# A fused recurrent, feed-forward and attention block on one core: a negative mean for GpSimd, five small loads on another queue, the weight preparation on VectorE, and a new plan

## The chip, the core and the metric

The kernel runs on one core of a Trainium2 chip. The core has five engines that work side by side: TensorE (PE, matrix products; its weight loads are shown as PEld), VectorE (DVE), ScalarE (ACT), GpSimd (POOL) and SyncE (SP), which here only issues transfers. The metric is the device time of one execution in microseconds (us): 1856.88 us is the median of three executions before the change (1855.34 to 1861.38).

## The reference

x has 4096 tokens of 256 channels in float32. Four residual layers follow one another, each on a layer-normalized x:

```
x = x + A(ln(x)); x = x + F(ln(x)); x = x + B(ln(x)); x = x + F(ln(x))

A(x): i, f, o = sigmoid(x Wi + bi), sigmoid(x Wf + bf), sigmoid(x Wo + bo);  s = tanh(x Ws + bs)
      h_t = f_t * h_(t-1) + i_t * s_t           (a scan over all 4096 tokens, per channel)
      z = x + o * h;  A = (z - mean z) / sqrt(var z + eps) * gamma + beta
F(x): p = x of the token before (0 for the first)
      r = sigmoid((mu_r x + (1 - mu_r) p) W_r);  k = (mu_k x + (1 - mu_k) p) W_k
      F = r * (relu(k)^2 W_v)
B(x): q, k, v = x Wq' + bq, x Wk' + bk, x Wv' + bv;  16 heads of 16 channels
      causal softmax(q k' / 4) v per head, over all earlier tokens;  B = that Wo' + bo
```

## The kernel before

The first three layers' token-wise part and the attention run interleaved. A **unit** is 256 tokens (16 of them, `UNIT`), a **chunk** 512 tokens (8). Each unit goes through normalization LN_X, the gates f, i, s, o, the scan, the normalization LN_Z, the first feed-forward (LN_F1) and the projections to q, k and v (LN_A); this is called the front here. Attention goes over 32 **steps**, four groups of four heads for each chunk. A step has two passes over its keys. In the first one (`max`), TensorE makes the scores of 128 queries against up to 512 keys and VectorE reduces each to its maximum (L1284). In the second one (`scores`, L1510), the scores come again with the maximum subtracted by two additional rows of the product (`shift`, `place`), ScalarE takes the exponential (`exp`, L1069) and TensorE adds up the values (`pv`, L1531). A step's scores can't begin before all its maxima are known. After a chunk's four steps its two units get the output projection and the second feed-forward (LN_F2).

**The order of the work** on each engine is written out when the program is built. `schedule()` plays the whole kernel through with a table of costs (`COST`), of landings (`LANDS`, `LOADED`) and with weights (`WORTH`) by which TensorE chooses between a maximum, a score, a `pv` and a product of a unit (`job`). An engine then executes its instructions in that fixed order and waits on semaphores for what they need. `MAX_AHEAD` and `AHEAD` say how far the maxima may run ahead of the scores (in steps, and in key columns; all maxima together have 540,672 columns). `LEAD` says how far the load of a unit may run ahead of the attention: `may_begin` lets the load of unit u start when the position in chunks plus LEAD plus 1 has reached u/2. `MOST` says how many of the seven PSUM banks each kind may hold.

**A normalization** (`normalize`, L843 to L848) has VectorE make mean and variance (L1143, L1158); GpSimd then makes rstd = (var + eps)^-0.5 in two small instructions (L840, L841, each waited for) and applies `(x - mean) * rstd` in two instructions of 128x256 (L846). For the first `EARLY` = 2 units of the front, and the last `LATE` = 2 of the second feed-forward, GpSimd makes only rstd and VectorE applies it (`apply` L1178, `z.apply` L1188 and L1194); for their feed-forward VectorE also subtracts (L1206) and accumulates (L1211), and ScalarE squares (L1023), where GpSimd does these three for the other units (L927, L937, L932).

**The preparation** is done once. GpSimd waits until all 15 transfers of `rest_loaded` have landed (the weights v, q, k, r, k of the feed-forward, v and o of the attention, five vectors of 256, and three broadcast rows), halves the weight w_v (L858), makes 1 - mu_r and 1 - mu_k (L860), bv as columns (L863) and the squares of the q and k weights (L866). TensorE sums the squares (L1452, `bound`) and makes the product of bv with w_ao (L1459, `bo`), VectorE adds that to bo (L1122, `bo.add`) and makes from the sums a scale for q and k (`scale.bound`, `scale.apply`). At the start SyncE's queue issues x of unit 0, the gate weights, two further units of x, then the other weights and rows. ScalarE's queue issues four gate biases, gamma and beta, and then the five vectors bq, bk, mu_r, mu_k and bv (L959) before ScalarE's first instruction.

Of the kernel before, what the change touches and what calls it, by code (L numbers as in the profile page):

```python
# [59 lines left out]
MOST = {"max": 4, "scores": 5, "job": 4}  # L60
# [9 lines left out]
EARLY = 2  # L70
# [3 lines left out]
def at_ends(u, ln):  # L74
    return u >= UNITS - LATE if ln == LAST else u < EARLY

# [6 lines left out]
          for a in range(0, (c * TT + qt + 1) * P, SPAN)]  # L83
# [3 lines left out]
AHEAD = 2212205  # L87
LEAD = 1.5
SOON, TWO = 0, -1300
REDUCE, EXP = 600, 480  # L90
WORTH = {"max": 2400, "dve": 1.0, "scores": 2650, "act": 1.562, "half": 450, "pv": 750, "stay": -4750, "two":
         -650, "ring": 900, "last": -2850, "job": 900, "age": 0.021, "same": 750, "after": -900, "rest": 450}
# [11 lines left out]
    "DVE": {"ln.stats": 660, "ln.mean": 140, "is": 620, "scan": 1320, "y": 700, "z": 620, "mixk": 750, "mixr": 750,  # L104
            "r*kv": 620, "q.part1": 800, "kk.part1": 800, "x3": 620, "neg": 230, "part0": 180, "part1": 180,
            "recip": 190, "norm": 350, "halve": 300, "scale.bound": 2300, "scale.apply": 3500,
            "bo.add": 400, "apply": 500, "z.apply": 1600, "subtract": 620, "accumulate": 620},
    "POOL": {"ln.norm": 2300, "z.norm": 4900, "rstd": 1100, "f.affine": 600, "x+beta": 1290, "diff": 1250, "k2": 1050,
             "x2": 1290, "x2+bo": 1290, "mask": 650, "scale.raise": 1100, "prev": 250, "consts": 6500, "prepare": 5000},
# [6 lines left out]
LOADED = {"halve": 9000.0, "f": 10000.0, "prepare": 20000.0}  # L116
# [6 lines left out]
def followed():  # L123
# [26 lines left out]
    op(("prepare",), ("consts",))  # L150
    op(("bound",), ("prepare",))
# [5 lines left out]
    for u in range(UNITS):  # L157
# [46 lines left out]
        for f in (FIRST, LAST):  # L204
# [18 lines left out]
            op(("kv", u, f, 0), ("square" if at_ends(u, f) else "k2", u, f), *so_on("kv", u - 1, f, 1))  # L223
# [32 lines left out]
def schedule():  # L256
# [15 lines left out]
    def offer(k):  # L272
        ready[engine[k[0]]][k] = max([seen[a] for a in after[k]] + [LOADED.get(k[0], 0.0)])

# [256 lines left out]
def build(nc, x, Wi, bi, Wf, bf, Wo_gate, bo_gate, Ws, bs, gamma, beta, WqT, bq, WkT, bk, WvT, bv, WoT, bo,  # L531
          WrT, WkfT, WvfT, mu_r, mu_k, out):
    with ExitStack() as ctx:
# [24 lines left out]
        small = sb("small", [P, 4 * 3 + 2 + 5 * UT * (6 + 2 + 2) + UT + CT * 3])  # L558
# [3 lines left out]
        var_eps, rstd = (small[:, 14 + n * UT:14 + (n + 5) * UT].rearrange("p (l t) -> p l t", l=5) for n in (40, 45))  # L562
        minus_half = small[:, 14 + 50 * UT:14 + 51 * UT]
        h_last = small[:, 14 + 51 * UT:14 + 51 * UT + CT].rearrange("p (k a) -> p k a", a=1)
# [144 lines left out]
        def _(sp):  # L709
# [8 lines left out]
            for n, w in (("v", WvfT), ("aq", WqT), ("ak", WkT), ("r", WrT), ("k", WkfT), ("av", WvT), ("ao", WoT)):  # L718
                matrix(n, w, rest_loaded)
# [851 lines left out]
```

## Time and profile before

| | |
|---|---|
| time, median of three | 1856.88 us |
| the profiled execution, its own time | 1857.59 us |
| its span, first to last instruction | 1855.9 us |
| busy, of the span | PE 1749.0 (94%), DVE 1583.7 (85%), ACT 1312.5 (71%), POOL 530.3 (29%) |
| granted TensorE clock, mean | 0.985 |

The time outside the span is 1.7 us. A row of a timeline has the start in us from the span's start, the length in us of the instructions merged in it, engine, line, operation, output and input, and in brackets the idle time of the engine just before and what ended it. An engine's name with a q (ACTq, SPq) is its queue issuing transfers. A busy PE is not a PE at its peak, since the ends of its products are modelled.

### The profile page before, as it was taken

How to read it: one execution, taken by the hardware profiler on the slowest of the kernel's cores; microseconds unless marked ns; L12 is line 12 of the kernel's file. 1: busy time of each engine (PE TensorE's matmuls, PEld its weight loads, DVE VectorE, ACT ScalarE, POOL GpSimd, SP SyncE). 2: the span in 40 equal slices, each digit the busy share in tenths (PEclk: the TensorE clock that was granted, in tenths of full speed). 3: DMA queues.
4: the chain of work that ended last, by engine and by line, in shares of the span. 5: the costliest groups of instructions: out<-in, count | busy, mean ns of one | idle time of the engine just before them, and what ended most of it. 6: DMA issues, size and time to landing. Idle time of an engine off the chain costs nothing.

```text
span 1855.9 us, 34235 instructions
## 1 busy us (share of the span) xinstructions
PE 1749.0 (94%) x12684; PEld 755.4 (41%) x12684; DVE 1583.7 (85%) x3175; ACT 1312.5 (71%) x2757; POOL 530.3 (29%) x655
## 2 busy tenths in 40 slices
PE   6689999999999999999999999999999999999997
PEld 5565546354444343353443333433432233332224
DVE  4566789897989998999999999999999999999802
ACT  2235474647676877748778878788778888888893
POOL 5556645544432232432213022131110001110001
PEclk9988999999999999999999999999999999999998
DMA  3131202121020000020002000000110000000000
GB/s 105 40 63 33 50 19 49 38 41 34 16 51 12 20 15 23 12 46 12 28 17 34 6 1 17 28 1 6 33 25 5 6 4 3 13 1 7 1 1 12
DMA packets 56954, 42.99 MB, mean 23 GB/s; under 512 B 8788, under 2 KB 56788, under 8 KB 56788
## 3 DMA queue, kind: packets, MB, share of 16 engines
q1 hardware_dynamic: 53188, 39.74, 8.8%
q10 hardware_dynamic: 3600, 1.06, 0.4%
q8 instruction: 101, 1.65, 0.4%
q14 instruction: 65, 0.53, 0.1%
HBM read 24.00 MB, written 16.25 MB: 22 GB/s over the span
## 4 chain that ended last, share of the span: by engine, by line
PE 29%; DVE 22%; ACT 6%; POOL 3%; issue 2%; DVEq 0%; POOLq 0%; ACTq 0%
DVE span_max L1284 19%; PE psum L1531 9%; PE psum L1510 6%; PE psum L1478 5%; ACT probs L1069 5%; PE psum L1347 4%; PE psum L1341 3%; POOL rows L846 1%; PE psum L1335 1%; DVE rows L1252 1%; DVE small L1143 0%; POOL small L841 0%; PE psum L1540 0%; PE psum L1485 0%; POOL probs L953 0%
## 5 line engine op out<-in xcount | busy, mean ns | idle before, releaser
L1284 DVE TENSOR_REDUCE span_max<-psum 128x1 f32<-128x512 f32 (+3 forms) x2304 | 1312.7, 635 | 73.4 <-PE psum L1478 36.4
L1069 ACT ACTIVATE probs<-psum 128x512 f32<-128x512 f32 (+3 forms) x2304 | 1115.5, 596 | 204.1 <-PE psum L1510 200.8
L1531 PE MATMUL psum<-probs,v_aug 128*17 128x512 f32 (+3 forms) x4608 | 569.2, 566 | 5.8 <-POOL probs L953 4.3
L1478 PE MATMUL psum<-k_stack,q_stack 48*128 48x512 f16 (+3 forms) x2304 | 520.0, 364 | 15.5 <-DVE span_max L1284 8.9
L1510 PE MATMUL psum<-q_stack,k_stack 50*128 50x512 f16 (+3 forms) x2304 | 515.5, 367 | 6.5 <-ACT probs L1069 1.5
L1510 PEld LDWEIGHTS psum<-q_stack,k_stack 50*128 50x128 f16 x2304 | 137.5, 93 | 510.9 <-ACT probs L1069 440.4
L953 POOL TENSOR_SCALAR_AFFINE_SELECT probs<-probs 128x512 f32<-128x512 f32 x128 | 82.0, 643 | 603.0 <-ACT probs L1069 602.9
L1478 PEld LDWEIGHTS psum<-k_stack,q_stack 48*128 48x128 f16 x2304 | 165.1, 94 | 197.4 <-DVE span_max L1284 111.3
L846 POOL TENSOR_SCALAR rows<-rows,small 128x256 f32<-128x256 f32 x140 | 174.3, 1253 | 7.4
L1531 PEld LDWEIGHTS psum<-probs,v_aug 128*17 128x17 f32 x4608 | 76.6, 95 | 137.6 <-issue 112.7
L995 ACT ACTIVATE rows<-psum,cols 128x256 f32<-128x256 f32 x128 | 53.6, 470 | 83.7 <-PE psum L1341 83.2
L937 POOL TENSOR_TENSOR rows<-rows 128x512 f32<-128x512 f32 x28 | 35.5, 1268 | 193.8 <-DVE rows L1261 193.8
L1485 PE MATMUL psum<-mask_keys,mask_rows 64*128 64x64 bf16 x1024 | 90.2, 190 | 0.0
L1143 DVE BATCH_NORM_STATS2 small<-rows 128x6 f32<-128x256 f32 x160 | 59.5, 414 | 33.9 <-POOL rows L906 23.7
L1335 PE MATMUL psum<-ident,rows 128*128 128x128 f32 x256 | 42.7, 294 | 47.1 <-POOL rows L846 23.1
L1485 PEld LDWEIGHTS psum<-mask_keys,mask_rows 64*128 64x128 bf16 x1024 | 74.7, 97 | 29.8 <-issue 0.8
L1341 PE MATMUL psum<-rows,w_k 128*128 128x256 f32 x256 | 73.0, 410 | 8.0 <-DVE rows L1252 6.6
L932 POOL TENSOR_TENSOR rows<-rows 128x512 f32<-128x512 f32 x28 | 29.6, 1058 | 170.7 <-ACT rows L1017 170.7
L1308 DVE RECIPROCAL inv_sum<-psum 128x16 f32<-128x16 f32 x32 | 8.1, 253 | 78.6 <-PE psum L1540 78.2
L1036 ACT ACTIVATE rows<-psum,cols 128x256 f16<-128x256 f32 x64 | 26.8, 471 | 64.0 <-PE psum L1341 63.8
L1347 PE MATMUL psum<-w_r,rows 128*128 128x256 f32 x256 | 70.4, 399 | 1.6 <-DVE span_max L1284 0.9
L1347 PE MATMUL psum<-w_v,rows 128*128 128x256 f32 x256 | 69.7, 396 | 2.1 <-POOL rows L932 0.7
(118 smaller groups left out, 1347.7 us busy)
## 6 DMA issues: line engine op xcount, KB each, us to landing
q_stack<-q_parts SPq DMA_DIRECT2D x192, 32.0 KB, 2.0
k_stack<-k_parts SPq DMA_DIRECT2D x42, 128.0 KB, 4.8
rows<-in_x SPq DMA_DIRECT2D x16, 256.0 KB, 3.0
q_parts<-rows SPq DMA_DIRECT2D x32, 128.0 KB, 1.9
k_parts<-rows SPq DMA_DIRECT2D x32, 128.0 KB, 2.0
out<-rows SPq DMA_DIRECT2D x16, 256.0 KB, 2.2
x_rows<-rows SPq DMA_DIRECT2D x14, 256.0 KB, 2.1
rows<-x_rows SPq DMA_DIRECT2D x14, 256.0 KB, 2.8
```

The source lines that it names most:

```text
L846: ins = nc.gpsimd.tensor_scalar(dst[:, j], src[:, j], mean_var[:, ln, j, 0:1], rstd[:, ln, j:j + 1], ALU.subtract, ALU.mult)
L953: nc.gpsimd.affine_select(out=tri, in_=tri, compare_op=ALU.is_ge, fill=0.0, base=0, pattern=[[0, HG], [1, P]], channel_multiplier=-1).then ...
L1069: act.activation(probs[:, tile % PROBS, i, q0:], bank(b)[:, q0:], ACT.Exp, scale=SCALE / QK_SCALE).then_inc(exp_done, 1)
L1143: ins = nc.vector.bn_stats(stats[:, ln, j], src[:, j])
L1284: nc.vector.tensor_reduce(span_max[:, s % SPAN_RING, row:row + 1, k0 // SPAN:k0 // SPAN + 1], bank(b)[:, 0:k1 - k0], AX.X, ALU.max).then_i ...
L1335: ins = nc.tensor.transpose(bank_chan(b)[:, k, j * P:(j + 1) * P], src[:, j, k * P:(k + 1) * P], ident[:])
L1341: ins = nc.tensor.matmul(bank_chan(b)[:, e], w[:, k, e * P:(e + 1) * P], src[:, k], start=(k == 0), stop=(k == CT - 1))
L1347: ins = nc.tensor.matmul(bank_tok(b)[:, j], src[:, k, j * P:(j + 1) * P], w[:, k], start=(k == 0), stop=(k == CT - 1))
L1478: ins = nc.tensor.matmul(bank(b)[:, 0:k1 - k0], q_stack[row:row + SCORE_ROWS, s % Q_RING, u, qt * P:(qt + 1) * P], k_stack[row:row + SCORE ...
L1485: ins = nc.tensor.matmul(bank(b)[:, k:k + HALF], mask_rows[row:row + HALF, n], mask_keys[row:row + HALF], start=False, stop=(n == 1))
L1510: nc.tensor.matmul(bank(b)[:, q0:], k_stack[row:row + STACK, g * PAIRS + u, j * P:(j + 1) * P], q_stack[row:row + STACK, s % Q_RING, u, q0 ...
L1531: ins = nc.tensor.matmul(pv_bank[32 * h:32 * h + VW, q0:], v_aug[:, j, g * HG + h, :], probs[:, tile % PROBS, h, q0:], start=(j == 0), sto ...
```

## The change

It has seven parts. (1) GpSimd's `normalize` gets an additional small instruction, neg_mean = -mean, and applies `(x + neg_mean) * rstd`. (2) The five vectors bq, bk, mu_r, mu_k, bv are issued by SyncE, after the weights of q, k and v, and no longer by ScalarE. SyncE issues the weights in the order aq, ak, v and then, after the vectors, r, k, av, ao. (3) The preparation moves from GpSimd to VectorE, in two parts, `prepare` and `halve.v`; the first product with w_v waits for the second. (4) `EARLY` goes from 2 to 4, so units 2 and 3 of the front are treated like 0 and 1. (5) The planner's costs and landings are new. (6) Its weights and limits are new: `LEAD` 1.5 to 8.5, `AHEAD` 2212205 to 40342, `MOST` of the jobs 4 to 3, and every entry of `WORTH`. (7) With 5 and 6, and with the new operations, every engine's order is planned anew.

```diff
-MOST = {"max": 4, "scores": 5, "job": 4}
+MOST = {"max": 4, "scores": 5, "job": 3}
-EARLY = 2
+EARLY = 4
-AHEAD = 2212205
-LEAD = 1.5
-SOON, TWO = 0, -1300
+AHEAD = 40342
+LEAD = 8.5
+SOON, TWO = 0, -300
-WORTH = {"max": 2400, "dve": 1.0, "scores": 2650, "act": 1.562, "half": 450, "pv": 750, "stay": -4750, "two":
-         -650, "ring": 900, "last": -2850, "job": 900, "age": 0.021, "same": 750, "after": -900, "rest": 450}
+WORTH = {"max": 2700, "dve": 1.0, "scores": 2500, "act": 1.25, "half": 150, "pv": 1950, "stay": -6100, "two":
+         400, "ring": -3150, "last": -4650, "job": 1500, "age": 0.008, "same": 300, "after": -750, "rest":
+         750}
...
-    "POOL": {"ln.norm": 2300, "z.norm": 4900, "rstd": 1100, "f.affine": 600, "x+beta": 1290, "diff": 1250, "k2": 1050,
-             "x2": 1290, "x2+bo": 1290, "mask": 650, "scale.raise": 1100, "prev": 250, "consts": 6500, "prepare": 5000},
+    "POOL": {"ln.norm": 2550, "z.norm": 5100, "rstd": 1100, "f.affine": 600, "x+beta": 1290, "diff": 1250, "k2": 1050,
+             "x2": 1290, "x2+bo": 1290, "mask": 650, "scale.raise": 1100, "prev": 250, "consts": 6800},
-LOADED = {"halve": 9000.0, "f": 10000.0, "prepare": 20000.0}
+LOADED = {("halve",): 6000, ("f", 0, 0): 10000, ("i", 0, 0): 10500, ("s", 0, 0): 11000, ("o", 0, 0): 11500,
+          ("ln.stats", 0, LN_X): 4400, ("ln.stats", 1, LN_X): 11600, ("ln.stats", 2, LN_X): 12500,
+          ("prepare",): 21000, ("halve.v",): 21000}
...
+    op(("halve.v",), normalized(0, LN_Z))
...
-            op(("kv", u, f, 0), ("square" if at_ends(u, f) else "k2", u, f), *so_on("kv", u - 1, f, 1))
+            op(("kv", u, f, 0), ("square" if at_ends(u, f) else "k2", u, f), ("halve.v",), *so_on("kv", u - 1, f, 1))
...
-            for n, w in (("v", WvfT), ("aq", WqT), ("ak", WkT), ("r", WrT), ("k", WkfT), ("av", WvT), ("ao", WoT)):
+            for n, w in (("aq", WqT), ("ak", WkT), ("v", WvfT)):
+                matrix(n, w, rest_loaded)
+            for n, v in (("aq", bq), ("ak", bk), ("mu_r", mu_r), ("mu_k", mu_k), ("av", bv)):
+                sp.dma_start(cols[:, COL[n], :], v.rearrange("(k p) -> p k", p=P),
+                             allow_slow_non_contiguous=True).then_inc(rest_loaded, 16)
+            for n, w in (("r", WrT), ("k", WkfT), ("av", WvT), ("ao", WoT)):
                 matrix(n, w, rest_loaded)
...
             def normalize(dst, src, ln):
+                nc.gpsimd.tensor_scalar(neg_mean[:, ln], mean_var[:, ln, :, 0], -1.0, None, ALU.mult)
                 settle(raised(ln))
                 for j in range(UT):
-                    ins = nc.gpsimd.tensor_scalar(dst[:, j], src[:, j], mean_var[:, ln, j, 0:1],
-                                                  rstd[:, ln, j:j + 1], ALU.subtract, ALU.mult)
+                    ins = nc.gpsimd.tensor_scalar(dst[:, j], src[:, j], neg_mean[:, ln, j:j + 1],
+                                                  rstd[:, ln, j:j + 1], ALU.add, ALU.mult)
...
-                elif op[0] == "prepare":
-                    pool.wait_ge(rest_loaded, 16 * 15)
-                    nc.gpsimd.tensor_scalar(weights["v"][:], weights["v"][:], 0.5, None, ALU.mult)
...
-            for n, v in (("aq", bq), ("ak", bk), ("mu_r", mu_r), ("mu_k", mu_k), ("av", bv)):
-                vector(n, v, rest_loaded)
...
+                elif op[0] == "prepare":
+                    dve.wait_ge(rest_loaded, 16 * 15)
+                    for src, dst in (("mu_r", "om_r"), ("mu_k", "om_k")):
+                        nc.vector.tensor_scalar(cols[:, COL[dst], :], cols[:, COL[src], :], -1.0, 1.0,
+                                                ALU.mult, ALU.add)
+                    dve.wait_ge(consts_ready, 5)
+                    for k in range(CT):
+                        nc.vector.tensor_scalar(bv_cols[:, k], ones, cols[:, COL["av"], k:k + 1], None, ALU.mult)
+                    for n, name in enumerate(("aq", "ak")):
+                        w = weights[name]
+                        ins = nc.vector.tensor_tensor(w_squared[:, n], w[:], w[:], ALU.mult)
+                    ins.then_inc(prepared, 1)
+                elif op[0] == "halve.v":
+                    dve.wait_ge(rest_loaded, 16 * 15)
+                    nc.vector.tensor_scalar(weights["v"][:], weights["v"][:], 0.5, None, ALU.mult).then_inc(v_halved, 1)
...
+                        if LAYER[u, f] == 0:
+                            pe.wait_ge(v_halved, 1)
```

## Rows read from the trace of the kernel before

**Rows 1.** The page's part 1: busy us (share of the span) and instructions, by engine.
```profile
PE 1749.0 (94%) x12684; PEld 755.4 (41%) x12684; DVE 1583.7 (85%) x3175; ACT 1312.5 (71%) x2757; POOL 530.3 (29%) x655
```

**Rows 2.** Windows: busy PE, PEld, DVE, ACT, POOL; PEclk, DMA share, GB/s.
```profile
0.00:93.00 93.00, 62.02 (x264) 49.91 (x265) 48.19 (x137) 25.14 (x54) 50.55 (x86) 0.93 0.25 73
93.00:186.00 93.00, 81.24 (x556) 56.40 (x555) 57.32 (x154) 40.23 (x93) 55.45 (x63) 0.89 0.24 49
186.00:928.00 742.00, 711.40 (x5224) 339.67 (x5224) 665.74 (x1382) 488.61 (x1053) 292.30 (x343) 0.99 0.12 29
928.00:1753.00 825.00, 806.99 (x6118) 277.74 (x6114) 798.52 (x1471) 684.96 (x1399) 124.27 (x151) 1.00 0.05 12
1753.00:1856.00 103.00, 87.39 (x532) 31.73 (x528) 13.92 (x35) 73.61 (x160) 7.68 (x14) 0.95 0.02 6
```

**Rows 3.** Source line L1284: the maxima; ns min/median/max, first and last start.
```profile
L1284 DVE TENSOR_REDUCE span_max<-psum x2304: 220/678/693, 113.3 to 1752.2; 128x1 f32<-128x512 f32 x180, 128x1 f32<-128x128 f32 x6, 128x1 f32<-128x384 f32 x3, 128x1 f32<-128x256 f32 x3
```

**Rows 4.** Timeline of ScalarE after the last maximum.
```profile
1761.01 60.34 ACT L1069 ACTIVATE probs<-psum 128x512 f32<-128x512 f32 x128
```

**Rows 5.** Timeline of GpSimd, 22 to 32 us.
```profile
22.67 2.50 POOL L846 TENSOR_SCALAR rows<-rows,small 128x256 f32<-128x256 f32 x2
25.25 1.51 POOL L858 TENSOR_SCALAR w_v<-w_v 128x512 f32<-128x512 f32 x1
...
30.40 1.08 POOL L898 TENSOR_TENSOR rows<-rows,beta_b 128x512 f32<-128x512 f32 x1
31.58 0.23 POOL L840 TENSOR_SCALAR small<-small 128x2 f32<-128x2 f32 x1
```

**Rows 6.** Timeline of VectorE, 25 to 37 us.
```profile
25.30 0.25 DVE L1158 BATCH_NORM_AGGREGATE small<-small 128x2 f32<-128x6 f32 x2
...
35.42 0.42 DVE L1122 TENSOR_TENSOR bo_b<-bo_b,psum 128x256 f32<-128x256 f32 x1 [8.34 <-PE psum L1459]
35.76 0.88 DVE L1188 SCALAR_TENSOR_TENSOR rows<-rows,small,gamma_b 128x256 f32<-128x256 f32 x2
```

**Rows 7.** Timeline of GpSimd and of VectorE, 84 to 88 us.
```profile
84.30 2.43 POOL L846 TENSOR_SCALAR rows<-rows,small 128x256 f32<-128x256 f32 x2
...
87.90 1.51 DVE L1178 TENSOR_SCALAR rows<-rows,small 128x256 f32<-128x256 f32 x2 [3.83 <-POOL small L841]
```

**Rows 8.** GpSimd's groups by form: busy us, mean ns of one, idle before.
```profile
L846 POOL TENSOR_SCALAR rows<-rows,small 128x256 f32<-128x256 f32 x140 | 174.3, 1253 | 7.4
...
L841 POOL TENSOR_TENSOR small<-small 128x2 f32<-128x2 f32 x80 | 59.3, 742 | 6.7
...
L840 POOL TENSOR_SCALAR small<-small 128x2 f32<-128x2 f32 x80 | 21.2, 265 | 168.9 <-DVE small L1158 153.9 <-DVE rows L1211 10.1 <-POOL rows L937 2.6
...
L910 POOL TENSOR_SCALAR rows<-rows 128x512 f32<-128x512 f32 x16 | 10.1, 631 | 11.8 <-ACT rows L995 10.6
```

**Rows 9.** VectorE's groups by form: busy us, mean ns of one, idle before.
```profile
L1178 DVE TENSOR_SCALAR rows<-rows,small 128x256 f32<-128x256 f32 x16 | 6.7, 459 | 6.5 <-POOL small L841 6.4
...
L1211 DVE TENSOR_TENSOR rows<-rows 128x512 f32<-128x512 f32 x4 | 2.8, 691 | 0.1
...
L1188 DVE SCALAR_TENSOR_TENSOR rows<-rows,small,gamma_b 128x256 f32<-128x256 f32 x4 | 1.7, 478 | 0.0
```

**Rows 10.** Timeline of ScalarE's and SyncE's queues at the start; last row: us to landing.
```profile
3.95 1.13 ACTq L959 DMA_DIRECT2D cols<-in_bq  x1
...
8.34 1.28 ACT L978 ACT_TABLE_LOAD   x1 [8.34 <-issue]
...
12.62 0.46 SPq L721 DMA_DIRECT2D probs<-in_bk  x1
...
probs<-in_bk SPq DMA_DIRECT2D x1, 128.0 KB, 6.4
```

**Rows 11.** Waits over the whole span: us in total, times, longest.
```profile
DVE small L1143 <- POOL rows L906: 23.7, 10, 7.0
PE psum L1335 <- POOL rows L846: 23.1, 16, 4.0
```

More of the change, by code:

```diff
@@ L103 @@
             "v.copy": 500, "shift.copy": 480, "oT": 490, "square": 480, "act.load_k": 2800},
-    "DVE": {"ln.stats": 660, "ln.mean": 140, "is": 620, "scan": 1320, "y": 700, "z": 620, "mixk": 750, "mixr": 750,
+    "DVE": {"ln.stats": 660, "ln.mean": 140, "is": 620, "scan": 1320, "y": 700, "z": 620, "mixk": 830, "mixr": 830,
             "r*kv": 620, "q.part1": 800, "kk.part1": 800, "x3": 620, "neg": 230, "part0": 180, "part1": 180,
-            "recip": 190, "norm": 350, "halve": 300, "scale.bound": 2300, "scale.apply": 3500,
-            "bo.add": 400, "apply": 500, "z.apply": 1600, "subtract": 620, "accumulate": 620},
-    "POOL": {"ln.norm": 2300, "z.norm": 4900, "rstd": 1100, "f.affine": 600, "x+beta": 1290, "diff": 1250, "k2": 1050,
-             "x2": 1290, "x2+bo": 1290, "mask": 650, "scale.raise": 1100, "prev": 250, "consts": 6500, "prepare": 5000},
+            "recip": 190, "norm": 350, "halve": 300, "prepare": 2400, "halve.v": 420, "scale.bound": 2300, "scale.apply": 3500,
+            "bo.add": 400, "apply": 740, "z.apply": 1800, "subtract": 660, "accumulate": 690},
+    "POOL": {"ln.norm": 2550, "z.norm": 5100, "rstd": 1100, "f.affine": 600, "x+beta": 1290, "diff": 1250, "k2": 1050,
+             "x2": 1290, "x2+bo": 1290, "mask": 650, "scale.raise": 1100, "prev": 250, "consts": 6800},
     "SP": {"load_x": 500, "store_x2": 500, "store_q": 1000, "store_k": 1000, "load_k": 2800, "load_q": 2800,
@@ L272, in offer @@
     def offer(k):
-        ready[engine[k[0]]][k] = max([seen[a] for a in after[k]] + [LOADED.get(k[0], 0.0)])
+        ready[engine[k[0]]][k] = max([seen[a] for a in after[k]] + [LOADED.get(k, 0.0)])
     def done(k, t):
@@ L662, in build @@
         q_stored, k_stored = sem("q_stored"), sem("k_stored")
-        halved, prepared, bound_read, bound_ready, bound_raised = (
-            sem(n) for n in ("halved", "prepared", "bound_read", "bound_ready", "bound_raised"))
+        halved, v_halved, prepared, bound_read, bound_ready, bound_raised = (
+            sem(n) for n in ("halved", "v_halved", "prepared", "bound_read", "bound_ready", "bound_raised"))
         qk_scaled, bo_ready, unit_placed = sem("qk_scaled"), sem("bo_ready"), sem("unit_placed")
@@ L855, in _ @@
                     constants()
-                elif op[0] == "prepare":
-                    pool.wait_ge(rest_loaded, 16 * 15)
-                    nc.gpsimd.tensor_scalar(weights["v"][:], weights["v"][:], 0.5, None, ALU.mult)
-                    for src, dst in (("mu_r", "om_r"), ("mu_k", "om_k")):
-                        nc.gpsimd.tensor_scalar(cols[:, COL[dst], :], cols[:, COL[src], :], -1.0, 1.0,
-                                                ALU.mult, ALU.add)
-                    for k in range(CT):
-                        nc.gpsimd.tensor_scalar(bv_cols[:, k], ones, cols[:, COL["av"], k:k + 1], None, ALU.mult)
-                    for n, name in enumerate(("aq", "ak")):
-                        w = weights[name]
-                        ins = nc.gpsimd.tensor_tensor(w_squared[:, n], w[:], w[:], ALU.mult)
-                    ins.then_inc(prepared, 1)
                 elif op[0] == "scale.raise":
```

17 lines of the change are left out of this document (8 added, 9 removed).

## The prediction

> **What bounds the kernel now.** I read the busy shares first [rows 1]. They name PE, at 94%, but its ends are modelled and say little. So the second view is the windows [rows 2], and the third the line of the maxima and the timeline behind them [rows 3, 4]. The last maximum starts at 1752.2 us and behind it comes a tail that nothing of this change shortens: ScalarE's exponentials run from 1761.0 for 60.3 us without a gap, and the last two units' output follows, to 1855.9. The tail is 1855.9 - 1753 = 103 us. Before it, from 928 to 1753, VectorE is busy 798.5 of 825 us (97%); from 186 to 928 it is 665.7 of 742 (90%); in the first 93 us 48.2, in the next 93 us 57.3. The maxima are VectorE's, each step's scores wait for them, and they start only at 113.3. So the time is: VectorE's work up to 1753 (48.2 + 57.3 + 665.7 + 798.5 = 1569.7), its idle time up to there (44.8 + 35.7 + 76.3 + 26.5 = 183.3), the tail (103), and 1.7 outside the span (1857.6 - 1855.9). A change pays where it takes idle time from VectorE, and work given to VectorE costs its full length unless it falls into idle time. Of the 183.3, 80.5 lie in the first 186 us, in which chains of small steps over four engines rule. Behind 186 PE shows 711.4 of 742 and 807.0 of 825: whoever wants VectorE fuller there must have PE choose the maxima at the right moment, which is the plan's matter.
>
> **The preparation leaves GpSimd.** Unit 0's statistics of LN_Z are ready at 25.30 + 0.25 = 25.55 [rows 6], but GpSimd begins their rstd at 31.58 [rows 5]. In between it ends a normalization of unit 2 (two instructions, 2.50 us), does the preparation (25.25 to 30.40, 5.15 us) and a beta addition (1.08). And VectorE, with `bo.add` ahead of it in its order, sits idle for 8.34 us until PE has made `bo` from the prepared columns, so that unit 0's `z.apply` starts at 35.76. Without both, rstd could begin at about 25.6 and, with its 0.27 + 0.74 = 1.0 us [rows 8] and 0.2 to be seen, `z.apply` at 26.8: 9.0 us sooner. Against it stands the work on VectorE: two instructions of 128x2, two of 128x128, two squares of 128x512 at 0.69 and w_v at no more than that [rows 9]. For the four small ones I take 0.25 each, half of L1178's 0.46 for 256 columns: 1.0 + 3 x 0.69 = 3.1 us. They have a place in the idle 8.3 us. The landing is the other term. The last one that `rest_loaded` waits for is now issued at 12.62 and lands 6.4 us later, at 19.0 [rows 10]; five issues that took ScalarE's queue from 3.95 to 8.34, 4.4 us, now go ahead of it on SyncE's, so I expect 23.4. If the plan puts `prepare` at 21 us, VectorE stands 2.4 us there, with unit 1's apply and unit 0's scan behind it. Bounds of this part: a gain of 9.0, and a loss of 4.4 if the landings delay the chain and the 9 us are covered by what else unit 0 needs. I take 9.0 - 2.4 = -6.6 us. The weights r, k, av and ao and the three rows are 4.4 us later too, covered by the same wait; the rows of ones for k_stack behind them on SyncE are read by the first scores only, behind the first maxima at 113.3, and cost nothing.
>
> **ScalarE's queue.** Its table load starts at 8.34, when the last issue ends [rows 10]; five issues less, it starts at 3.95 and is over at 5.2. It stood ahead of the first copy of unit 0, so the gain is between 0 (that copy's input comes later, or the gates wait for weights and biases anyway) and its whole length of 1.28. I take -0.5.
>
> **EARLY 4.** For units 2 and 3 four applications of two instructions each leave GpSimd, 4 x 2 x 1.253 = 10.0 us a unit, with LN_Z's two additions, the difference, the square and the sum. VectorE gets six instructions at 0.459, four at 0.478, two at 0.69 [rows 9]: 2.8 + 1.9 + 1.4 = 6.1 a unit, 12.2 in all. They fall between 20 and 170 us, inside the idle 80.5. How much of it stays covered? Beside GpSimd's work the apply pair at 87.90 took 1.51 where the mean is 0.92 [rows 7, 9]. So it may be up to 12.2 x 1.51/0.92 = 20. I charge a quarter of 12.2, +3; the bounds are 0 and +20. The gain: a norm of unit 2 stands on GpSimd ahead of unit 1's rstd of LN_A, and VectorE waits 3.83 us for that rstd, until 87.90 [rows 7]. With EARLY 4 the 2.43 us of applying and most of its rstd's 1.0 are gone from there: -3.4. Unit 1 is the last that the first maxima need, so -6.6, -0.5 and -3.4 add up: the first maximum at 113.3 - 10.5 = 103. From there to 186 GpSimd's norms keep PE and VectorE waiting (23.1 and 23.7 us over the run, 26 waits [rows 11]); units 2 and 3 have two thirds of the front's steps there, and I take -3 for them, between 0 and -8.
>
> The Trainium skill (GPSIMD Engine Reference, section 1, the table, and section 8) has GpSimd share its SBUF interfaces with VectorE, to the harm of instructions with two SBUF inputs or in a two-port mode. The trace agrees at 87.90. By that rule at its worst the charge of +3 above would be +20 and the sum smaller by 17; I keep the +3, since the idle time around it is not used up.
>
> **The negative mean.** An application costs 1.253 us for 256 columns with subtract and multiply, while L910, a multiply and an add by constants, has 0.631 for 512 [rows 8]. What add and multiply cost with two columns of scalars no row shows. Bounds: 0.32 (L910's rate) and 1.25 (no change). I take 0.6, nearest to L910 with some fixed part; with it the norm is 0.27 + 0.74 + 0.27 + 1.2 = 2.5, which is also what the new cost table says (2550). A norm on GpSimd gets shorter by 2 x 0.65 - 0.27 = 1.0 us, 62 of them; if the rate stays, longer by 0.27. GpSimd is busy 29% [rows 1], so only those norms count that somebody waits for. Of the 26 waits [rows 11] ten are VectorE's and each is over 1 us in the mean: 10 x 1.0, of which I take half because PE is full there, -5 (bounds +2 and -15).
>
> The same reference (section 3.1) gives a body of up to two operations 1.03 cycles per element at 1.2 GHz, an estimate of 0.22 us for 256 elements besides the fixed part. The 1.253 of the subtracting form disagrees with it, L910's 0.631 for 512 is near it. By the rule the norm would fall by 1.8 instead of 1.0 and the term be -9.
>
> **The new plan.** The weights and LEAD change every engine's order behind 186 us. The tail is the same sequence, so it is 0 there. LEAD 8.5 sets no limit any more (unit 15 needs 7.5), AHEAD 40342 is over one step of the last chunk (31,232 columns) and the maxima are just in time there, so it does nothing in the mean. A maximum is worth 2700 less VectorE's backlog, a job 1500 + 0.008 ns per ns of age: a job of 50 us age wins when the backlog is over 800 ns; before it won from 450 ns on (900 + 1050 against 2400). So aged jobs interrupt VectorE's supply less. Against that LEAD lets the front, which needs PE more than VectorE, crowd into the middle, where VectorE stands 76.3 us already. The idle time between 186 and 928 can't fall below the 3% of the later stretch (-52), and I take +40 as the other end, half as much idle time again. My value is -4, near zero since both effects are real and neither is measured.
>
> **Sum.** 1857.6 - 6.6 - 0.5 - 3.4 - 3 + 3 - 5 - 4 = 1838.1, against a profiled execution that is 0.7 above the median; I predict 1838 us. Under 0.3%, 5.6 us, is what a measurement of this kernel can't tell from no change.
>
> **Rivals.** (A) LEAD starves VectorE, slower. With no gate at 7.5, units 6 to 15 are loaded as soon as their buffers are free; their products fill PE, at 711 of 742 us already, and maxima come late. For it: VectorE's 90% in the middle against 97% later, when fewer units are there. Against it: a maximum still outbids a job below a backlog of 0.8 to 1.2 us. Price: at an idle share of 15% instead of 10.3% between 186 and 928 +35 us, less 5 in the later stretch: 1842 + 30 = 1872, without the plan's -4. It decides from 13% on, where the +20 eat the other terms. (B) The start is covered. PE has to do the front's work anyway and shows 81 of 93 us from 93 on, so maxima that begin 10 us sooner are followed by a longer wait for chunk 1; only the norms' -5 and half of the plan's remain, and the extra work of +3: 1853 to 1857, no change. For it: VectorE idles 35.7 us after 93 though maxima have begun. Against it: those waits name GpSimd's norms. (C) The plan pays. If the middle's idle share falls to 6%, that is -32 instead of -4: 1810. For it: better costs (a norm was planned at 2300 and takes about 3.5), so orders that fit what happens. Against it: the late stretch is at 97% and has nothing to give.
>
> **How the numbers follow.** The forecast, 1828 to 1850, has 0.46; (C) 0.20; (B) 0.14; (A) 0.20. Faster by over 0.3% is the forecast and (C), and a little of (B): 0.67; within 0.3% 0.13; slower (A) 0.20. The range is 1814 to 1866: its low end holds most of (C), its high end the milder half of (A).
>
> **What would show it.** The first maximum (L1284) at 100 to 106 instead of 113.3; `z.apply` of unit 0 at 27 to 30; no wait of VectorE for `bo` of 8 us; the norm's two instructions near 0.6 us each, 124 of them; idle time of VectorE before the last maximum of 160 to 170 us, with 15 us more work; the last maximum near 1735 and the tail still 103. Wrong it would be if VectorE's idle time between 186 and the last maximum grew by over 15 us (A), if the first maximum came sooner and the last did not (B), or if the adding form took 1.25 us.

## The result and the profile after

The changed kernel takes 1813.66 us (median of four runs, 1811.92 to 1814.18) against 1858.95 for the kernel before beside it (median of four): a ratio of 0.9757, with a 95% interval from 0.974 to 0.9775. That is 45 us or 2.4% faster. I had forecast 1838, with a range down to 1814. In the experiments below, one run of n_sub and one of the kernel before (beside b_true) ran at a much lower granted clock, 0.843 and 0.557, and took longer; both are left out.

The page of the changed kernel, part 1:
```profile
PE 1743.2 (96%) x12684; PEld 755.9 (42%) x12684; DVE 1594.4 (88%) x3206; ACT 1314.2 (73%) x2759; POOL 426.7 (24%) x684
```

VectorE has 10.7 us more work than before [rows 1] in a span that is 43.5 us shorter, and GpSimd has 104 us less. The windows, with the last two cut where the changed kernel's last maximum ends (stretch and its us, then busy us of PE, PEld, DVE, ACT, POOL, then PEclk, DMA share, GB/s):
```profile
0.00:93.00 93.00, 68.05 (x288) 55.01 (x289) 59.47 (x166) 27.58 (x60) 34.35 (x70) 0.93 0.27 75
93.00:186.00 93.00, 87.67 (x620) 60.41 (x618) 70.19 (x193) 44.08 (x105) 46.86 (x76) 0.94 0.29 62
186.00:928.00 742.00, 732.46 (x5502) 338.31 (x5499) 688.51 (x1406) 529.46 (x1136) 225.78 (x356) 1.00 0.12 27
928.00:1711.00 783.00, 768.06 (x5752) 270.86 (x5750) 762.13 (x1407) 639.37 (x1299) 112.01 (x169) 1.00 0.05 12
1711.00:1812.00 101.00, 86.97 (x532) 31.36 (x530) 14.09 (x36) 73.74 (x160) 7.69 (x14) 0.95 0.02 6
```

The reader is to take VectorE's idle time from them, stretch minus DVE, and set it beside [rows 2]. It is 33.5 instead of 44.8 in the first 93 us, 22.8 instead of 35.7 in the next 93, 53.5 instead of 76.3 from 186 to 928, and 20.9 instead of 26.5 from there to the last maximum. The sum is 130.7 instead of 183.3. With the work before the last maximum (1580.3 instead of 1569.7) it ends at 1711 instead of 1753, and the tail is 101 us instead of 103: 52.6 - 10.6 + 2 = 44 us. This sum closes by construction, since it only splits the span; what it shows is where the time went, and the forecast was wrong on how much idle time goes.

The maxima, and GpSimd's instructions of a norm (L854 the negative mean, L850 and L851 rstd, L857 the application), to set beside [rows 3] and [rows 8]:
```profile
L1293 DVE TENSOR_REDUCE span_max<-psum x2304: 252/682/716, 108.6 to 1710.5; 128x1 f32<-128x512 f32 x180, 128x1 f32<-128x128 f32 x6, 128x1 f32<-128x384 f32 x3, 128x1 f32<-128x256 f32 x3
```
```profile
L857 POOL TENSOR_SCALAR rows<-rows,small 128x256 f32<-128x256 f32 x124 | 70.2, 573 | 6.8
...
L851 POOL TENSOR_TENSOR small<-small 128x2 f32<-128x2 f32 x80 | 60.4, 755 | 6.7
...
L850 POOL TENSOR_SCALAR small<-small 128x2 f32<-128x2 f32 x80 | 19.8, 248 | 64.8 <-DVE small L1167 60.7
...
L854 POOL TENSOR_SCALAR small<-small 128x2 f32<-128x2 f32 x62 | 16.7, 270 | 166.0 <-DVE small L1167 153.4 <-DMA x_rows<-rows 8.1 <-POOL rows L936 2.5
```

The first maximum starts at 108.6, 4.7 us earlier and not the 10.5 that I had summed up. An application takes 573 ns instead of 1253. And the waits for GpSimd's norms are mostly gone. VectorE's for LN_Z's result, 23.7 us in [rows 11], is the first line. Of PE's for an application, 23.1 us, no line is left; the second line is the only wait for an application, and it is VectorE's:
```profile
DVE small L1152 <- POOL rows L905: 5.4, 1, 5.4
DVE small L1167 <- POOL rows L857: 0.8, 1, 0.8
```

### The profile page after: what moved, and what is told of

Its sections match the earlier page's. It is cut to its first block, busy times and chain, and to the rows that moved or that the text cites. A ratio compares the mean times of both kernels' runs of the same rounds, so it can differ in the third digit from the quotient of the medians.

```text
span 1812.4 us, 34297 instructions
## 1 busy us (share of the span) xinstructions
PE 1743.2 (96%) x12684; PEld 755.9 (42%) x12684; DVE 1594.4 (88%) x3206; ACT 1314.2 (73%) x2759; POOL 426.7 (24%) x684
## 3 DMA queue, kind: packets, MB, share of 16 engines
q10 hardware_dynamic: 2240, 1.05, 0.4%
## 4 chain that ended last, share of the span: by engine, by line
PE 37%; DVE 22%; ACT 6%; issue 2%; POOL 0%; DVEq 0%; ACTq 0%; POOLq 0%
DVE span_max L1293 20%; PE psum L1542 12%; PE psum L1521 7%; PE psum L1489 7%; ACT probs L1063 5%; PE psum L1356 5%; PE psum L1350 5%; PE psum L1344 1%; PE psum L1551 0%; DVE small L1152 0%; PE psum L1496 0%; DVE rows L1234 0%; ACT oT L1070 0%; PE psum L1504 0%; DVE rows L1286 0%
## 5 line engine op out<-in xcount | busy, mean ns | idle before, releaser
L1489 PE MATMUL psum<-k_stack,q_stack 48*128 48x512 f16 (+3 forms) x2304 | 538.1, 364 | 8.7 <-DVE span_max L1293 4.9
L1521 PEld LDWEIGHTS psum<-q_stack,k_stack 50*128 50x128 f16 x2304 | 143.4, 93 | 498.8 <-ACT probs L1063 423.6
L936 POOL TENSOR_TENSOR rows<-rows 128x512 f32<-128x512 f32 x26 | 33.0, 1268 | 215.3 <-DVE rows L1270 215.3
L857 POOL TENSOR_SCALAR rows<-rows,small 128x256 f32<-128x256 f32 x124 | 70.2, 573 | 6.8
L1261 DVE SCALAR_TENSOR_TENSOR rows<-rows,cols 128x256 f32<-128x256 f32 x128 | 63.6, 542 | 0.1
L1344 PE MATMUL psum<-ident,rows 128*128 128x128 f32 x256 | 42.4, 291 | 21.9 <-DVE rows L1187 19.4
```

Source lines behind the costliest of these rows:

```text
L857: ins = nc.gpsimd.tensor_scalar(dst[:, j], src[:, j], neg_mean[:, ln, j:j + 1], rstd[:, ln, j:j + 1], ALU.add, ALU.mult)
L1261: ins = nc.vector.scalar_tensor_tensor(out=dst[:, k], in0=xr[:, k], scalar=cols[:, COL[om], k:k + 1], in1=xT[:, k, 1:], op0=ALU.mult, op1= ...
L1344: ins = nc.tensor.transpose(bank_chan(b)[:, k, j * P:(j + 1) * P], src[:, j, k * P:(k + 1) * P], ident[:])
L1489: ins = nc.tensor.matmul(bank(b)[:, 0:k1 - k0], q_stack[row:row + SCORE_ROWS, s % Q_RING, u, qt * P:(qt + 1) * P], k_stack[row:row + SCORE ...
L1521: nc.tensor.matmul(bank(b)[:, q0:], k_stack[row:row + STACK, g * PAIRS + u, j * P:(j + 1) * P], q_stack[row:row + STACK, s % Q_RING, u, q0 ...
```

## The experiments

All times are medians of four runs (n_sub: three, worth_old: ten), each beside runs of the kernel before, which had 1857.3 to 1858.6 in the five sets. Two theories stood at first: O, the new instructions carry the gain, and P, the new order of the work does.

**1. The changed kernel with the slow norm (n_sub), in the same order.**
```diff
-                nc.gpsimd.tensor_scalar(neg_mean[:, ln], mean_var[:, ln, :, 0], -1.0, None, ALU.mult)
-                    ins = nc.gpsimd.tensor_scalar(dst[:, j], src[:, j], neg_mean[:, ln, j:j + 1],
-                                                  rstd[:, ln, j:j + 1], ALU.add, ALU.mult)
+                    ins = nc.gpsimd.tensor_scalar(dst[:, j], src[:, j], mean_var[:, ln, j, 0:1],
+                                                  rstd[:, ln, j:j + 1], ALU.subtract, ALU.mult)
```


> The changed kernel with every engine's order as it is, but GpSimd's normalization subtracts the mean again (no negative mean, 124 applications in the slow form, 573 ns becomes about 1253). A norm is 1.1 us longer (2 x 0.68 - 0.25), 62 of them. Theory P (the new order of the work carries the gain): 1816 to 1824 us. Theory O (the new instructions carry it, because shorter norms feed VectorE): 1835 us or more.

Measured: 1835.6 us, ratio to before 0.9884 (0.9855 to 0.9912). The slow norm costs 21.9 us in the changed kernel's order, as theory O has it, and the rest of the change keeps 21.7 us.

**2. The kernel before with the negative mean alone (b_add), in the order of before.** The edit is the reverse of the one above, in before's code, with room for the negative mean in `small`.

> The kernel before in its own order, with the negative mean alone: 140 applications at about 573 ns instead of 1253. By the term of my forecast 1853 us (-5); theory P 1848 to 1857; theory O 1830 to 1842.

Measured: 1820.93 us, ratio 0.9802 (0.9783 to 0.9821), a gain of 36.4 us. It is the whole gain but for 7 us (1820.9 against 1813.7), from one instruction of 128x2 added to each of the 70 norms and one operation exchanged in their 140 applications. The order of every engine is otherwise the same as before, so the two traces can be read against each other. Windows of b_add:
```profile
0.00:93.00 93.00, 64.55 (x274) 52.19 (x275) 52.18 (x140) 25.11 (x55) 47.38 (x92) 0.93 0.25 73
93.00:186.00 93.00, 84.62 (x606) 60.15 (x604) 63.53 (x164) 44.59 (x106) 54.99 (x84) 0.96 0.31 60
186.00:928.00 742.00, 731.18 (x5384) 348.44 (x5385) 690.68 (x1427) 505.10 (x1089) 242.65 (x382) 1.00 0.12 28
928.00:1717.00 789.00, 774.03 (x5895) 262.93 (x5892) 766.87 (x1411) 662.39 (x1349) 101.64 (x154) 1.00 0.05 12
```
VectorE's idle time from 186 to 928 is 51.3 us instead of 76.3 [rows 2], 25 us less, and PE's is 10.8 instead of 30.6. I also took the distance between the two traces at every 64th of the 2304 maxima. The first is 3.2 us earlier, the one of 194 us 10.9, that of 357 us 19.7, that of 564 us 26.1, that of 850 us 33.6, that of 1240 us 35.7, and from there to the last it stays at 35.7. The saving comes in small steps as long as units of the front are under way, and at most 1 us of it is given back on the way. The waits of b_add, in the order of VectorE for LN_Z, PE for an application, ScalarE for the copy that stands behind the norms in GpSimd's queue, VectorE for an application:
```profile
DVE small L1145 <- POOL rows L908: 11.9, 3, 6.1
PE psum L1337 <- POOL rows L848: 8.4, 4, 3.3
ACT small L1009 <- POOL rows L920: 5.9, 5, 3.1
DVE small L1160 <- POOL rows L848: 0.8, 1, 0.8
```
The same four in the kernel before are the two of [rows 11] and these, where the row of ScalarE is one that I hadn't counted:
```profile
ACT small L1007 <- POOL rows L918: 15.4, 7, 4.0
...
DVE small L1158 <- POOL rows L846: 1.8, 1, 1.8
```
They sum to 64.0 us before and 27.0 in b_add: 37 us less, and the kernel is 36.4 us faster. These four are a choice, though. More waits name GpSimd, whose work stands behind norms in its queue: PE's for the masked probabilities, VectorE's for rstd, for f and for the difference. With every wait of VectorE, ScalarE and TensorE that names GpSimd (but for the identity matrix at the start) the four comparisons that change the norm alone in one fixed order read so, in us (n_sub is experiment 1; experiments 3 and 6 describe b_half and b_params):

| order of | edit | the four waits | all waits for GpSimd | time saved |
|---|---|---|---|---|
| before | to b_add | 64.0 to 27.0: 37.0 | 98.6 to 47.0: 51.6 | 36.4 |
| before | to b_half | 64.0 to 51.9: 12.1 | 98.6 to 79.9: 18.7 | 15.3 |
| the changed kernel | n_sub to the changed one | 26.8 to 6.8: 20.0 | 48.8 to 22.5: 26.3 | 21.9 |
| b_params | to b_add_params | 29.3 to 12.4: 16.9 | 78.9 to 41.2: 37.7 | 41.2 |

The four waits fit in three rows and miss the last by more than half. The fall of all waits is 0.9 to 1.4 of the time saved in every row: it gives the size, not the number, and that waits pass through one for one isn't shown. The last row is also the one in which the mean granted clock moved most, from 0.973 to 0.985.

Part of the gain may go by way of TensorE's clock. In the kernel before, the granted clock is at its lower level (0.50 of full speed, 1.2 of 2.4 GHz) from 160.5 to 170 us, after PE had been busy for 6.0 of 10 us; in b_add it is at the upper one there, after 8.4 of 10 us. And the eight products that sum the squares of the weights ran at either level. The two windows and the two rows, the kernel before first in each pair:
```profile
160.50:170.00 9.50, 9.50 (x68) 4.30 (x68) 5.17 (x13) 5.26 (x12) 1.55 (x3) 0.50 0.10 33
160.00:170.00 10.00, 10.00 (x60) 7.20 (x53) 5.36 (x16) 6.06 (x16) 5.47 (x9) 1.00 0.10 27
```
```profile
30.59 3.49 PE L1452 MATMUL psum<-probs 128*128 128x256 f32 x8 [2.52 <-POOL probs L866]
30.36 1.96 PE L1454 MATMUL psum<-probs 128*128 128x256 f32 x8 [1.23 <-POOL probs L868]
```
The mean granted clock of the profiled executions is 0.985 before and 0.991 in b_add. By my estimate from them, the lower level took (1 - 0.985) x 1855.9 = 28 us off the one and (1 - 0.991) x 1818.9 = 16 off the other, so up to about 11 of the 36.4 us may have come by the clock, if PE's work bounded every such stretch. No run holds the clock fixed, so how the gain is divided between fewer waits and a higher clock stays open; that the norm's length brought it is shown.

**3. Half of the gain (b_half), in the order of before.**
```diff
...
+                ins = nc.gpsimd.tensor_scalar(dst[:, 0], src[:, 0], neg_mean[:, ln, 0:1],
+                                              rstd[:, ln, 0:1], ALU.add, ALU.mult)
+                ins = nc.gpsimd.tensor_scalar(dst[:, 1], src[:, 1], mean_var[:, ln, 1, 0:1],
+                                              rstd[:, ln, 1:2], ALU.subtract, ALU.mult)
```


> The kernel before in its own order, with the negative mean, but only the first of a norm's two applications adds; the second subtracts as before. A norm is 0.4 us shorter (0.67 - 0.25) instead of 1.1. If the time follows the norm's length (36.4 us for 1.09): 1843 us (-14). If the gain needs the norm to get under a threshold, either about 1857 or about 1822.

Measured: 1843.26 us, ratio 0.9924 (0.9908 to 0.9939), where 1843 was worked out. In this order the time follows the norm's length, about 35 us per us of norm, as if half of the 70 norms counted. In the changed kernel's order it is 21.9 us for 1.1, about 20 per us with 62 norms. The two forms stand side by side in its trace:
```profile
L849 POOL TENSOR_SCALAR rows<-rows,small 128x256 f32<-128x256 f32 x70 | 88.4, 1263 | 0.0
...
L847 POOL TENSOR_SCALAR rows<-rows,small 128x256 f32<-128x256 f32 x70 | 39.8, 569 | 7.6
```

**4. Is it the plan's mistake about the norm?** The plan of before charges 2300 ns for a norm that takes about 3500. Two kernels were planned with the true length and keep the slow norm: the one before (b_true), and n_sub (n_sub_true).
```diff
-    "POOL": {"ln.norm": 2300, "z.norm": 4900, "rstd": 1100, "f.affine": 600, "x+beta": 1290, "diff": 1250, "k2": 1050,
+    "POOL": {"ln.norm": 3600, "z.norm": 6200, "rstd": 1100, "f.affine": 600, "x+beta": 1290, "diff": 1250, "k2": 1050,
```


> The kernel before, planned with what a norm on GpSimd takes in its trace (ln.norm 3600 instead of 2300, z.norm 6200 instead of 4900), all instructions as they are. Theory M (the stalls come from the plan's mistake: engines are ordered behind norms that end 1.2 us later than planned): most of the 36 us comes back, 1825 to 1840 us. Theory L (a slow norm costs its length in any order): 1850 to 1866 us.

> The changed kernel with the subtracting norm, as n_sub (1836.2 us), but planned with its true cost of 3600 and 6200 us/1000. Theory M: 1812 to 1824 us. Theory L: 1830 to 1842 us.

Measured: 1876.96 (ratio 1.0103, 1.0083 to 1.0122) and 1845.55 (0.9935, 0.992 to 0.9951). Both are slower than with the wrong charge, by 19 and 10 us, where theory M wanted them faster: these two orders, made with the slow norm known, don't hide it. What a new order does by accident (next) is not much less than the 10.

**5. How much a new order does by accident (b_pace, pace_a).** `PACE = 1.05` becomes 1.051 in the kernel before and in the changed one.

> The kernel before, with PACE 1.051 instead of 1.05 in the planner, which stands for no change of any duration but gives another order. It shows how much a new order moves the time by accident. I expect within 8 us of before on either side, 1849 to 1866 us; if it moves by 15 us or more, no single run of a new plan shows the effect of its parameters.

> The changed kernel with PACE 1.051 instead of 1.05. If its plan is a fortunate one among equals, this is slower, 1818 to 1830 us; if its parameters carry the gain, within 4 us of 1813.7.

Measured: 1865.47 (ratio 1.0041, 1.0025 to 1.0057) and 1819.26 (0.9794, 0.9776 to 0.9813): 7 and 5.5 us slower. So a difference of 7 us between two planned kernels says nothing of a parameter. With one try each, how far an accident can go is not known.

The first of them shows where such a difference can lie. In b_pace the last maximum starts 4.2 us sooner than before [rows 3], and the kernel is slower all the same, because the tail is longer. Its maxima, and ScalarE behind the last one, to set beside [rows 4]:
```profile
L1284 DVE TENSOR_REDUCE span_max<-psum x2304: 227/678/693, 115.3 to 1748.0; 128x1 f32<-128x512 f32 x180, 128x1 f32<-128x128 f32 x6, 128x1 f32<-128x384 f32 x3, 128x1 f32<-128x256 f32 x3
```
```profile
1752.59 14.77 ACT L1069 ACTIVATE probs<-psum 128x512 f32<-128x512 f32 x35
...
1771.09 57.47 ACT L1069 ACTIVATE probs<-psum 128x512 f32<-128x512 f32 x122
```
ScalarE has 35 exponentials of the step before left where the kernel before has 11, and comes to the last long run 10 us later. From the start of the last maximum to the end of the span it is 113.9 us in b_pace, 103.7 before and 101.9 in the changed kernel, but 109.5 in plan_old, 109.4 in lead_old, 106.3 in early2 and 109.2 in b_add_early4 (102.4 in b_add). So 44% to 85% of what these four lose against the changed kernel or b_add, and all that b_pace loses, lies behind the last maximum, and the sum by VectorE's idle time alone can't see it.

**6. The plan's values (plan_old, b_params, b_add_params, b_add_cost).** plan_old is the changed kernel with every planner value of before. The others take the new `WORTH`, `TWO`, `LEAD`, `AHEAD` and `MOST` into the kernel before, then into b_add, and then add the new costs and landings. Two of the values; the others are those of the change:
```diff
-LEAD = 1.5
-SOON, TWO = 0, -1300
+LEAD = 8.5
+SOON, TWO = 0, -300
...
```


> The changed kernel's instructions (negative mean, EARLY 4, preparation on VectorE, loads on SyncE), but planned with the costs, landings, weights, LEAD, AHEAD and bank limits of the kernel before. Theory P: most of the 45 us is gone, 1838 to 1852 us. Theory O: 1815 to 1828 us.

> The kernel before, with the changed kernel's WORTH, TWO, LEAD, AHEAD and bank limit alone; costs, landings and all instructions of before. Theory P: 1820 to 1840 us. Theory O: 1850 to 1862 us. If the weights only pay with the right costs, it is in between or worse than before.

> The order of b_params (the kernel before with the new weights and LEAD, 1881.5 us), instruction by instruction, with the negative mean added. If a shorter norm is worth more where more units crowd into the first half, it gains more than the 36 us it gave in the order of before: 1815 to 1840. If it is worth the same 36: 1845. If the new weights and LEAD are bad in themselves with the old costs, it stays above 1840.

> b_add_params (negative mean, new weights and LEAD, EARLY 2, preparation on GpSimd, loads on ScalarE's queue; 1840.4 us) with the new costs and landings in addition. The same with the preparation on VectorE is early2 at 1822.9. If the costs make the difference between the two: 1820 to 1828. If the preparation on VectorE does: 1835 to 1843.

Measured:

| kernel | us | ratio to before (interval) |
|---|---|---|
| plan_old | 1828.71 | 0.9848 (0.9827 to 0.9868) |
| b_params | 1881.54 | 1.0128 (1.0108 to 1.0149) |
| b_add_params | 1840.38 | 0.9904 (0.9889 to 0.9919) |
| b_add_cost | 1824.85 | 0.9817 (0.9802 to 0.9832) |

The plan's values are worth 15 us beside the new instructions (1828.7 to 1813.7), twice the accident; plan_old itself lies just above what theory O allowed and well below theory P. On b_add the whole new plan gives nothing: 1824.9 against 1820.9. The new weights with the old costs are a loss of 24 us on the kernel before and of 19.5 on b_add; with the costs added 15.5 of these come back. b_params and b_add_params have one order and differ in the norm alone: 41.2 us. In three orders it was worth 36.4, 21.9 and 41.2.

**7. One value of the plan undone in the changed kernel: LEAD 1.5 (lead_old), the old weights (worth_old), the old costs (cost_old).**

> The changed kernel with LEAD 1.5 and everything else new. Rival A of my forecast (LEAD starves VectorE) says that this is faster than the changed kernel, 1795 to 1808 us; if the open LEAD helps, because VectorE finds more to do early, 1822 us or more; within 6 us of 1814 it is an accident of order.

> The changed kernel with the old WORTH and TWO, new costs and LEAD 8.5. If the weights matter by holding VectorE's supply (a job that has waited long wins less often): 1825 to 1840 us, with more idle time of VectorE before the last maximum. If LEAD and the costs carry the gain: 1814 to 1822.

> The changed kernel, planned with the costs and landings of before, new weights and LEAD. If the new weights only pay together with the new costs: 1830 to 1842 us, as b_add_params (1840.4) against b_add (1820.9). If the costs carry nothing: 1811 to 1822.

Measured: 1830.65 (ratio 0.9849, 0.9833 to 0.9866), 1856.93 (0.9995, 0.9981 to 1.0009), 1817.9 (0.9787, 0.977 to 0.9803). The open LEAD is good for 17 us beside the new weights. With the old weights the kernel looks like what my rival A feared; the window of worth_old:
```profile
186.00:928.00 742.00, 720.12 (x5054) 353.58 (x5051) 642.68 (x1342) 470.35 (x1020) 257.76 (x402) 0.98 0.13 30
```
VectorE stands 99.3 us in it, where the changed kernel has 53.5 and before 76.3 [rows 2]. That it is LEAD which does it is argued only: the nearest kernel with LEAD 1.5 and the old weights is plan_old, 28 us faster, and it differs in the costs and in `MOST` too. The costs of before are 4 us slower there, which is inside the accident. `AHEAD` needed no run: with 2212205 in its place the planner gives the very same order, so it does nothing.

**8. EARLY (early2, b_add_early4), the start (halve_late), the loads (loads_act).** early2 is the changed kernel with EARLY 2, b_add_early4 is b_add with EARLY 4, both planned anew. halve_late has `("halve",): 8300` in `LOADED`, which exchanges two neighbours in VectorE's order and nothing else. loads_act has the five vectors on ScalarE's queue and the weights in their old order on SyncE's.

> The changed kernel with EARLY 2, so units 2 and 3 of the front go back to GpSimd, planned anew. My forecast had EARLY 4 at -6.4 + 3: 1817 us. With an accident of the new order of about 6 us: 1812 to 1826. If EARLY 4 carries nothing, 1814 to 1820; if the start is what it was made for, first maximum 3 us later.

> The kernel before with the negative mean and EARLY 4, old plan values. The changed kernel loses 9.2 us with EARLY 2 again. If EARLY 4 is worth that in itself: 1812 us against b_add's 1820.9. If it is an accident of order: 1815 to 1830. If units 2 and 3 on VectorE cost it more than they free (12 us of work): 1826 to 1833, which would also explain why plan_old, with EARLY 4 and old values, is 8 us behind b_add.

> The changed kernel with one exchange in VectorE's order at the start: unit 0's first application goes ahead of the halving of the gate biases, which waits for their landing (8.23 us in the trace; application at 8.48 instead of 6.67). Everything else keeps its order. If the 1.8 us go through to the first maximum and to the end: 1811.5 to 1812.5; if the gates wait for something else anyway, 1813.7.

> The changed kernel in its order, with the five vectors back on ScalarE's queue and the weights in the old order on SyncE's. My forecast gave the move -0.5 us for the table load and +2.4 for later landings. The table load starts at 8.3 again instead of 4.0 and the first copy, which was at 10.63, doesn't wait for it: 1812 to 1815 us; if the landings or the table load count, 1816 to 1818.

Measured: early2 1822.9 (0.9811, 0.9796 to 0.9826), b_add_early4 1829.38 (0.9845, 0.9829 to 0.9861), halve_late 1812.68 (0.9754, 0.974 to 0.9769), loads_act 1813.69 (0.9758, 0.974 to 0.9776). EARLY 4 is worth 9.2 us under the new plan and costs 8.5 under the old, both near the accident; it has no price of its own. The loads are worth nothing: with them back in their old place the first maximum comes at 105.7, 2.9 us sooner than in the changed kernel, and the time is the same. halve_late shows a wait that the change brought in. In the changed kernel the halving of the biases stands ahead of unit 0's first application, waits for a landing, and the application starts at 8.48 instead of before's 6.7:
```profile
8.23 0.33 DVE L1086 TENSOR_SCALAR cols<-cols 128x2 f32<-128x2 f32 x3 [2.64 <-DMA cols<-in_bo_gate]
8.48 0.88 DVE L1187 TENSOR_SCALAR rows<-rows,small 128x256 f32<-128x256 f32 x2
```
and in halve_late:
```profile
6.53 0.74 DVE L1187 TENSOR_SCALAR rows<-rows,small 128x256 f32<-128x256 f32 x2 [1.25 <-POOL small L851]
8.16 0.31 DVE L1086 TENSOR_SCALAR cols<-cols 128x2 f32<-128x2 f32 x3 [0.89 <-DMA cols<-in_bo_gate]
```
The application comes 1.95 us sooner. The first maximum comes at 104.1 instead of 108.6, by more than that, and I did not trace the rest; the last one starts at 1707.5 instead of 1710.5. At the end the medians differ by 1.0 us and the ranges overlap, so halve_late is not shown to beat the changed kernel, and an earlier first maximum is not passed on in full.

## Why the prediction was wrong, step by step

**The balance** (VectorE's work, its idle time, the tail) closes on the changed kernel to within 1 us, as a split of the span must. The tail was right within 2 us, but its reason, "the same sequence, so it is 0 there", was not: other plans of the same work have tails of up to 113.9 us. VectorE's work grew by 10.6 us where I had 15. The signs don't agree with each other either: a last maximum near 1735 with 15 us more work leaves 1735 - 1585 = 150 us of idle time, not the 160 to 170 that I wrote; 130.7 was measured.

**The negative mean: the term that failed.** I priced an application at 0.6 us (573 ns measured) and the norm at 1.0 shorter (1.1), so the size of the operation was right. Then I put down -5 us, from "ten are VectorE's", halved "because PE is full there". Measured alone it is -36.4, in the changed kernel's order -21.9. The words that failed are "only those norms count that somebody waits for": true, but I counted them on VectorE only. PE waited for an application 16 times, ScalarE 7 times behind a norm in GpSimd's queue, and "PE is full there" overlooked 30.6 us of idle PE from 186 to 928 [rows 2]. In a fixed order a stall of any of the three engines can delay what follows on it. The waits of all engines for GpSimd, 98.6 us in the trace of before, had room for the gain; they fell by 51.6, the time by 36.4, and a part of up to 11 may have come by TensorE's clock. My bound of -15 was no bound, since it left PE and ScalarE out. GpSimd's 29% of the span was no argument either: b_half and b_add show each microsecond of a norm to weigh about 35 in the time. The other price in the forecast, 0.22 us for an application and -9 for the term, missed as well: an application takes 573 ns.

All 70 norms together are shorter by 70 x 1.1 = 77 us, and half of that came through; in the changed kernel's order 62 x 1.1 = 68, and a third. I know these shares only from the runs; no row of before gives them.

**The start.** I had -6.6, -0.5 and -3.4 ahead of the first maximum, 10.5 in all; it came 4.7 us sooner. The negative mean alone gives 3.2 of them in b_add, though hardly at unit 0: its rstd starts at 31.36 instead of 31.58, since the preparation stands between the norm of unit 2 and it. `bo.add` comes 1.8 us sooner, behind the eight products that ran at the higher clock, and unit 1's application 2.1 (85.82 instead of 87.90), behind the norm that I had priced there. That leaves 1.5 us for the preparation, the loads and EARLY 4 together, if they simply add. `z.apply` of unit 0 starts at 32.18, not at 27 to 30:
```profile
27.30 0.68 DVE L1247 SCALAR_TENSOR_TENSOR rows<-psum,rows 128x512 f32<-128x512 f32 x1
...
31.84 0.42 DVE L1131 TENSOR_TENSOR bo_b<-bo_b,psum 128x256 f32<-128x256 f32 x1 [1.25 <-PE psum L1470]
32.18 0.87 DVE L1197 SCALAR_TENSOR_TENSOR rows<-rows,small,gamma_b 128x256 f32<-128x256 f32 x2
```
Its z (L1247) is at 27.30 instead of 23.78, since unit 0's gates were 3.3 us late already: "it stood ahead of the first copy" was right for the table load (4.00 instead of 8.34), but the copy waited for the application, and that for the halving. In halve_late i * s (L1225) starts at 17.86 instead of 20.66 and `z.apply` at 29.38 instead of 32.18, so this one exchange is 2.8 of the 3.3 us, and of them nothing that can be told from no change is left at the end. The wait for `bo` fell from 8.34 us to 1.25, as forecast. The landing behind the moved loads I set at 23.4; VectorE's `prepare` started at 25.59 behind other work and had no wait. loads_act measures the loads at 0.0. The larger mistake is to have booked the first maximum's gain in full for the end: it is at 108.6 in the changed kernel, 105.7 in loads_act, 105.2 in cost_old, 104.1 in halve_late and 116.4 in early2, and the times are 1813.7, 1813.7, 1817.9, 1812.7 and 1822.9.

**EARLY 4**, at -6.4 and +3, can't be called right or wrong: -9.2 in one plan, +8.5 in another, with an accident of 5.5 to 7.

**The new plan**: -4 was too small by 11, measured beside the new instructions (15 us; on b_add it was nothing). Rival A's idle time showed only with the old weights (worth_old, +43 us). That the arithmetic of the job's age against VectorE's backlog decides, which I gave as the reason against it, fits but isn't shown, since `WORTH` was exchanged as a whole. I took LEAD for the harmful half, and beside the new weights it is worth 17 us, 7.5 of them in the tail. Rival C named the right result, 1810, with "the plan pays"; its size was right and its cause was not, since between half (21.9 of 45) and four fifths (36.4) of the gain are the norm's, depending on the order of work in which it is measured.

## What to carry to other kernels

Where engines run in a fixed order, price a shorter instruction by every engine that waits for it or for what stands behind it in its queue, not by the bounding engine's own waits. The sum of all these waits is a rough ceiling for what there is to win. How much of it falls is known only from a run: in the order of before it fell by half, and the time saved was 0.7 to 1.1 of the fall in four comparisons. An engine at 29% can hold 2% of the time. And before a planner's value is credited, plan once more with a value that means nothing: here that moved the time by 5.5 to 7 us, more than the loads, `AHEAD` or, in the changed kernel, the new costs were worth. Where the plan changes, look at the tail by itself.

## What the runs showed of the hardware

On GpSimd the two-operation instruction with two columns of scalars takes 1228 ns in the median as subtract and multiply, and 558 ns as add and multiply, at the same 128x256 float32 (1253 and 585 as means of before and b_add). The granted clock moved with the stalls: 0.89 from 93 to 186 us before, 0.96 in b_add in the same order, 1.00 instead of 0.99 from 186 to 928, as means over stretches at either level. The same eight products took 3.49 us at the lower level and 1.96 at the upper.

The Trainium skill (GPSIMD Engine Reference, section 1) has GpSimd share its SBUF interfaces with VectorE, against instructions with two SBUF inputs or in a two-port mode. In the applications no harm showed in the mean, 458 ns after and 459 before [rows 9]. L1252's 495 ns for two operands became 542 in the changed kernel (512 in b_add, 505 in lead_old, 512 in cost_old), at most 6 us of VectorE's 10.7 us of additional work. GpSimd itself was busy for 104 us less there, and no run shows that it is the cause.
